# Quantising the ternary layer: two steps of the input rows put on ScalarE, the scaling of the activations on GpSimd, three copies reordered

## What is computed

```python
def _bitlinear(x, w):
    rms = jax.lax.rsqrt(jnp.maximum(jnp.mean(w * w), EPS))
    w_quant = jnp.clip(jnp.round(w * rms), -1.0, 1.0) / rms
    scale = 127.0 / jnp.maximum(jnp.max(jnp.abs(x), axis=-1, keepdims=True), EPS)
    x_quant = jnp.clip(jnp.round(x * scale), -128.0, 127.0) / scale
    return jnp.einsum('bsd,fd->bsf', x_quant, w_quant)
x = x + _bitlinear(gelu(_bitlinear(_layernorm(x), w1)), w2)     # w1: 1024 x 256, w2: 256 x 1024
```

## Time and profile before

| what | value |
|---|---|
| median of 3 runs | 1510.41 us |
| the profiled execution's own time | 1510.13 us |
| its span in the profile | 1508.3 us |
| mean granted TensorE clock, share of full speed | 0.992 |
| span in which the changed lines run | about 1112 to 1160 us |

### The profile page before, as it was taken

The page is one execution under the profiler, slowest core; times in us unless marked ns, Lnnn a source line. Parts: engine busy times, 40 slices in busy tenths (PEclk is TensorE's granted clock), DMA queues, the critical chain, the costliest instruction groups (busy, mean ns, idle before and its releaser), DMA issues. The chain is left out here.

```text
span 1508.3 us, 22223 instructions
## 1 busy us (share of the span) xinstructions
PE 1430.7 (95%) x6910; PEld 1028.8 (68%) x6910; DVE 891.3 (59%) x1934; ACT 768.1 (51%) x2122; POOL 528.0 (35%) x519
## 2 busy tenths in 40 slices
PE   3999998999989999999999999999997999999998
PEld 1678777788875556557878888876764666665656
DVE  7898988898975342323454545354677555553322
ACT  4888888899973211110234444444457555554210
POOL 2667577877762000000434242422110333331000
PEclk9999999999999999999999999999999999999999
DMA  5211000200005511112100000000232000011120
GB/s 202 73 51 60 8 5 2 96 2 1 2 1 220 217 51 51 54 49 91 67 1 1 1 1 1 15 15 1 107 143 102 1 1 1 1 30 42 46 68 18
DMA packets 21303, 71.65 MB, mean 48 GB/s; under 512 B 3858, under 2 KB 6290, under 8 KB 18244
## 3 DMA queue, kind: packets, MB, share of 16 engines
q1 hardware_dynamic: 12980, 57.37, 10.2%
q10 hardware_dynamic: 8208, 12.87, 2.7%
HBM read 69.01 MB, written 1.22 MB: 47 GB/s over the span
## 5 line engine op out<-in xcount | busy, mean ns | idle before, releaser
L1189 ACT ACTIVATE l0f_silu<-bank 128x512 f32<-128x512 f32 x48 | 28.5, 597 | 199.8 <-PE bank L1113 189.7
L827 POOL TENSOR_TENSOR l0a_stepped<-l0a_y,l0a_m 128x512 f32<-128x512 bf16 x64 | 73.9, 1154 | 91.5 <-DVE l0a_m L575 90.4
L1292 DVE TENSOR_TENSOR l0f_product<-l0f_silu,bank 128x512 f32<-128x512 f32 x48 | 32.9, 688 | 123.4 <-ACT l0f_silu L1189 123.3
L855 POOL TENSOR_TENSOR l0a_head_rstd<-l0a_head_var,all_minus_half 128x4 f32<-128x4 f32 x96 | 99.7, 1043 | 7.6 <-DVE l0a_head_var L597 7.6
L767 ACT ACTIVATE l0a_work<-bank,l0a_neg_max 128x128 f32<-128x128 f32 x256 | 90.2, 370 | 1.0 <-DVE l0a_neg_max L610 0.9
L1125 PEld LDWEIGHTS bank<-all_weights_a,l0f_hidden 128*128 128x128 f32 x384 | 72.9, 190 | 25.2 <-issue 17.0
L1721 DVE TENSOR_TENSOR all_weights_a<-bank,all_cols 128x512 f32<-128x512 f32 x64 | 43.9, 690 | 77.9 <-PE bank L1556 45.9
L427 PEld LDWEIGHTS bank<-l0a_k_t,l0a_q_t 128*128 128x128 f32 x512 | 64.0, 191 | 36.7 <-ACT l0a_q_t L753 31.3
L1125 PE MATMUL bank<-all_weights_a,l0f_hidden 128*128 128x256 f32 x384 | 88.9, 379 | 0.0
L2314 PE MATMUL bank<-l3a_f_xn_t,all_weights_b 128*128 128x512 f32 x192 | 86.2, 593 | 0.0
L800 ACT ACTIVATE l0a_work<-l0a_work,l0a_row_inv 128x128 f32<-128x128 f32 x256 | 82.3, 409 | 6.8 <-DVE l0a_row_inv L614 6.7
(11 more groups left out here) (437 smaller groups left out, 3754.1 us busy)
## 6 DMA issues: line engine op xcount, KB each, us to landing
l0f_spread<-l0f_weights ACTq DMA_DIRECT2D x32, 192.0 KB, 2.7
all_weights_a<-in_l_w_q SPq DMA_DIRECT2D x2, 2048.0 KB, 14.3
l0f_spread<-l0f_weights ACTq DMA_DIRECT2D x32, 128.0 KB, 2.8
all_weights_b<-in_l_e_gate_up SPq DMA_DIRECT2D x1, 3200.0 KB, 10.3
all_weights_b<-in_l_e_gate SPq DMA_DIRECT2D x1, 3072.0 KB, 10.0
all_weights_a<-in_l_e_up SPq DMA_DIRECT2D x4, 768.0 KB, 7.0
all_weights_a<-in_l_e_down SPq DMA_DIRECT2D x1, 3072.0 KB, 15.4
l3a_spread<-l3f_weights SPq DMA_DIRECT2D x10, 256.0 KB, 3.5
```

What stands on the lines that cost most here:

```text
L827: done = g.tensor_tensor(stepped[:, 0:n], value, step, ALU.add)
L855: g.tensor_tensor(head_rstd[:, m % 2, :], head_var[:, m % 2, :], res.minus_half[:, 0:HU], ALU.pow)\
```

## The change

ACT gets two steps of `round_in`, for all four pairs (ACT_PAIRS is TILES // 2, which is PAIRS): `normalise_in` (scale rstd, bias -mean x rstd) and `scale_in`. POOL gets the activations' `scale_act`, and the two small scales, and it makes the bias, for which DVE negates the mean. DVE's `round_in` is cut in two, `step_in` (maxima, step, inverse) and a rest. The turning and copying of pairs 2 and 3 are moved forward on PE and ACT, ahead of copies of values, and a one-element Gelu is run early on ACT so that the table of that function is loaded there.

```diff
 PE
                 if t == 3:
                     project_l3_values(6)
+                    turn_in(2)
                     project_l3_values(7)
-                if t % 2 == 1 and t // 2 + 1 < PAIRS:
-                    turn_in(t // 2 + 1)
+                if t == 4:
+                    turn_in(3)
 ACT
             def gelu(t):
-                act.wait_ge(in_q_ready, t // 2 + 1)
+                act.wait_ge(in_scale_ready, t // 2 + 1)
-            def scale_act(t):
-                act.wait_ge(act_inv_ready, t + 1)
-                act.activation(act_rows[t % 4], act_rows[t % 4], ACT.Identity, bias=magic[:],
-                               scale=act_inv[:, t:t + 1]).then_inc(act_scaled, 1)
+            def normalise_in(p):
+                act.wait_ge(in_rstd_ready, p + 1)
+                for t in (2 * p, 2 * p + 1):
+                    done = act.activation(in_rows[:, t, :], res.x[:, t, :], ACT.Identity, bias=in_offset[:, t:t + 1],
+                                          scale=in_rstd[:, t:t + 1])
+                done.then_inc(in_normed, 1)
+            def scale_in(p):
+                act.wait_ge(in_inv_ready, p + 1)
+                if p >= 1:
+                    act.wait_ge(in_q_ready, p)
+                for t in (2 * p, 2 * p + 1):
+                    done = act.activation(in_round[:, t % 2, :], in_rows[:, t, :], ACT.Identity, bias=magic[:],
+                                          scale=in_inv[:, t:t + 1])
+                done.then_inc(in_rounded, 1)
+            act.activation(spare[:], res.minus_half[:, 0:1], ACT.Gelu)
             norm_mix(0)
...
+            normalise_in(0)
+            scale_in(0)
             keep_l3_values(3)
+            normalise_in(1)
             keep_l3_values(4)
+            scale_in(1)
             keep_in(0)
             gelu(0)
+            normalise_in(2)
             keep_in(1)
             gelu(1)
             keep_l3_values(5)
+            scale_in(2)
             for t in range(TILES + 1):
-                if t < TILES:
-                    scale_act(t)
                 if 2 <= t + 2 < TILES:
                     gelu(t + 2)
                 if t == 0:
+                    normalise_in(3)
+                if t == 1:
+                    keep_in(2)
                     keep_l3_values(6)
                     keep_l3_values(7)
                 if t >= 1:
                     keep_act(t - 1)
-                if t % 2 == 1 and (t + 3) // 2 < PAIRS:
-                    keep_in((t + 3) // 2)
+                if t == 1:
+                    scale_in(3)
+                if t == 2:
+                    keep_in(3)
 DVE
+                if p < ACT_PAIRS:
+                    v.tensor_scalar(in_neg[:, pair], res.moments[:, pair, 0], -1.0, None, ALU.mult)
+            def step_in(p):
+                v.wait_ge(in_normed, p + 1)
+                v.tensor_reduce(in_max[:, pair], in_rows[:, pair, :], X, ALU.max, apply_absolute_value=True)
+                v.drain()
+                v.tensor_scalar(in_step[:, pair], in_max[:, pair], T_EPS, 1.0 / 127.0, ALU.max, ALU.mult)
+                v.drain()
+                v.reciprocal(in_inv[:, pair], in_step[:, pair]).then_inc(in_inv_ready, 1)
+            def round_in(p):
+                v.wait_ge(in_rounded, p + 1)
                 if p >= 2:
                     v.wait_ge(in_turned, p - 1)
                 v.tensor_scalar(in_q[:, p % 2, :, :], in_round[:], ROUND_INT, 127.0, ALU.subtract, ALU.min).then_inc(in_q_ready, 1)
-                v.tensor_scalar(act_scale[:, t:t + 1], act_step[:, t:t + 1], ternary.rms[:, 1:2], None, ALU.mult)
             add_to_x(1)
+            step_in(0)
+            open_gate(3)
             round_in(0)
-            open_gate(3)
+            step_in(1)
             add_to_x(2)
             round_in(1)
             add_to_x(3)
+            step_in(2)
             for t in range(TILES + 3):
                 ...
-                if t % 2 == 0 and t // 2 + 2 < PAIRS:
-                    round_in(t // 2 + 2)
+                if t == 0:
+                    round_in(2)
+                    step_in(3)
+                if t == 1:
+                    round_in(3)
 POOL
+            def scale_act(t):
+                g.wait_ge(act_inv_ready, t + 1)
+                g.tensor_scalar(act_rows[t % 4], act_rows[t % 4], act_inv[:, t:t + 1], ROUND_INT, ALU.mult, ALU.add)\
+                 .then_inc(act_scaled, 1)
+            in_rstd_of(0)
+            in_rstd_of(1)
+            in_scale_of(0)
+            in_rstd_of(2)
+            in_scale_of(1)
+            in_rstd_of(3)
+            in_scale_of(2)
+            for t in range(TILES):
+                scale_act(t)
+                act_scale_of(t)
+                if t == 0:
+                    in_scale_of(3)
+                if t == NEXT_MOMENTS:
+                    g.wait_ge(next_var_ready, 1)
+                    g.tensor_tensor(next_rstd[:], next_var[:], res.minus_half[:, 0:1], ALU.pow).then_inc(next_rstd_ready, 1)
```

More of the change, by code:

```diff
@@ L2725, in layer1_adapters_to_layer2 @@
         in_scale = mem.sb("in_scale", [TILES])
+        in_neg = mem.sb("in_neg", [TILES])
+        in_offset = mem.sb("in_offset", [TILES])
+        spare = mem.sb("spare", [1])
+        ACT_PAIRS = TILES // 2
         in_round = mem.sb("in_round", [2, D])
@@ L2784, in layer1_adapters_to_layer2 @@
         in_q_ready = mem.sem("mid_in_q_ready")
+        in_normed = mem.sem("mid_in_normed")
+        in_inv_ready = mem.sem("mid_in_inv_ready")
+        in_rounded = mem.sem("mid_in_rounded")
+        in_scale_ready = mem.sem("mid_in_scale_ready")
+        act_scale_ready = mem.sem("mid_act_scale_ready")
         in_turned = mem.sem("mid_in_turned")
@@ L3372, in add_to_x @@
                 pair = slice(2 * p, 2 * p + 2)
+                if p < ACT_PAIRS:
+                    v.tensor_scalar(in_neg[:, pair], res.moments[:, pair, 0], -1.0, None, ALU.mult)
                 v.tensor_scalar(in_var[:, pair], res.moments[:, pair, 1], T_EPS, None, ALU.add).then_inc(in_var_ready, 1)
[L3375 to L3379, removed]
+            def step_in(p):
+                pair = slice(2 * p, 2 * p + 2)
+                if p < ACT_PAIRS:
+                    v.wait_ge(in_normed, p + 1)
+                else:
+                    v.wait_ge(in_rstd_ready, p + 1)
+                    row_pair(in_rows, in_rstd, p)
+                    v.drain()
                 v.tensor_reduce(in_max[:, pair], in_rows[:, pair, :], X, ALU.max, apply_absolute_value=True)
@@ L3383, in round_in @@
                 v.drain()
[L3384 to L3389, removed]
+                v.reciprocal(in_inv[:, pair], in_step[:, pair]).then_inc(in_inv_ready, 1)
+            def round_in(p):
+                if p < ACT_PAIRS:
+                    v.wait_ge(in_rounded, p + 1)
+                else:
+                    v.drain()
+                    for t in (2 * p, 2 * p + 1):
+                        v.tensor_scalar(in_round[:, t % 2, :], in_rows[:, t, :], in_inv[:, t:t + 1], ROUND_INT, ALU.mult, ALU.add)
+                    v.drain()
                 if p >= 2:
@@ L3490, in _, with in_rstd_of, in_scale_of, act_scale_of @@
                  .then_inc(rstd_ready, 1)
-            for p in range(PAIRS):
+            def in_rstd_of(p):
                 pair = slice(2 * p, 2 * p + 2)
                 g.wait_ge(in_var_ready, p + 1)
-                g.tensor_tensor(in_rstd[:, pair], in_var[:, pair], res.minus_half[:, pair], ALU.pow).then_inc(in_rstd_ready, 1)
-            g.wait_ge(next_var_ready, 1)
-            g.tensor_tensor(next_rstd[:], next_var[:], res.minus_half[:, 0:1], ALU.pow).then_inc(next_rstd_ready, 1)
+                done = g.tensor_tensor(in_rstd[:, pair], in_var[:, pair], res.minus_half[:, pair], ALU.pow)
+                if p < ACT_PAIRS:
+                    g.drain()
+                    done = g.tensor_tensor(in_offset[:, pair], in_neg[:, pair], in_rstd[:, pair], ALU.mult)
+                done.then_inc(in_rstd_ready, 1)
+            def in_scale_of(p):
+                g.wait_ge(in_inv_ready, p + 1)
+                for t in (2 * p, 2 * p + 1):
+                    done = g.tensor_tensor(in_scale[:, t:t + 1], in_step[:, t:t + 1], ternary.rms[:, 0:1], ALU.mult)
+                done.then_inc(in_scale_ready, 1)
+            def act_scale_of(t):
+                g.wait_ge(act_inv_ready, t + 1)
+                g.tensor_tensor(act_scale[:, t:t + 1], act_step[:, t:t + 1], ternary.rms[:, 1:2], ALU.mult)\
+                 .then_inc(act_scale_ready, 1)
+            def scale_act(t):
+                g.wait_ge(act_inv_ready, t + 1)
+                g.tensor_scalar(act_rows[t % 4], act_rows[t % 4], act_inv[:, t:t + 1], ROUND_INT, ALU.mult, ALU.add)\
[15 more added lines that the diff above has]
+                    g.tensor_tensor(next_rstd[:], next_var[:], res.minus_half[:, 0:1], ALU.pow).then_inc(next_rstd_ready, 1)
 PLACES = {
```

1 line of the change is left out of this document (added).

## The result

Eleven timed executions of the changed kernel have the median 1514.54 us (1511.95 to 1516.78), eleven of the kernel before beside them 1510.44 (1509.95 to 1513.03). The ratio is 1.0022, with a 95% interval of 1.0013 to 1.0031: 3.3 us longer, 2.0 to 4.7 (the two medians are 4.1 apart). The profiled execution of the changed kernel took 1512.61 us with a span of 1510.5; that is 2.5 above the profiled execution of before, and among the shorter of the eleven.

The account below looks back on a forecast made before the run. Three engines were taken as nearly full, DVE the fullest. Waits of 8.4 us less 7.7 of removed work gave +0.7, the clock 0.3: 1510.13 + 1.0 = 1511.1 us, range 1506.5 to 1515.0.

Parts of the forecast that it names:

- What DVE loses: Normalising, rounding and in_scale of four pairs and eight act_scale leave DVE, four negated means come: net 7.7 us less.
- The six waits: DVE waits for ACT at round_in(0), step_in(1), step_in(2), round_in(2), step_in(3) and round_in(3): 8.4 us added.
- The ring: Before round_in(3): ACT's scale_in(3) stands behind keep_act(0), which needs DVE's finish_act(0); DVE waits 3.1 us.
- The sign that was named: DVE idle before L3380 and in_q in all four pairs, 8 to 9 us together, longest at pair 3, released by ACT.
- The clock: PE at its lower clock after longer idling makes narrow(0) late for DVE's first add_narrow: up to 0.75 us, taken as 0.3.
- POOL's scaling: The activations' scaling on POOL takes 1.1 us a tile, fitting within one tile's interval of DVE, 2.6 us.
- the third rival: POOL and DVE shut each other out (mutual exclusion); if POOL starts first, +8 us over eight tiles: 1518, chance 0.11.
- The exclusion: At finish_act(t-1) and POOL's scaling of tile t, both released by one inverse: whichever starts first holds up the other.
- the deciding 0.16 us: DVE starts a chained instruction 0.08 us after the last one's start, POOL 0.24 after it, so finish_act starts first.
- Costed at nothing: Forward moves of turn_in and the copies of pairs 2 and 3, and the early Gelu's table load: 0 us.
- the hidden waits: Rival: DVE's waits for ACT mostly hidden, half of them going: 3.5 us gained, 1506.6; chance 0.15.
- Slow POOL: Rival: POOL's scaling at its upper bound, 2.7 us a tile with the small scale, against DVE's 2.6: 1513.8; chance 0.08.

Follow-up runs that it names:

- ring: Changed kernel with ACT's scale_in(3) moved ahead of keep_in(2), so no longer behind keep_act(0); ratio to the kernel before 0.9996 (0.9987 to 1.0006).
- port_swap: Changed kernel with DVE's add_narrow(t-3) put between the inverse and finish_act(t-1); by the ratio +6.3 us (4.4 to 8.3) against the kernel before.
- moves_only: Kernel before with only the forward moves of turn_in and keep_in for pairs 2 and 3; by the ratio +0.8 us (-0.6 to 2.1).
- after_again: The changed kernel run and profiled once more, no edit; median 1515.34 us, kernel before 1512.81, ratio 1.002.
- order: Changed kernel with ACT's list reordered and two DVE steps one tile later, same instructions; median 1507.01 us, ratio to the kernel before 0.997.
- order_rows: `order` with DVE's normalise_next moved ahead of finish_act(3); by the ratio -4.1 us (-5.7 to -2.6) against the kernel before.
- pool_only: Kernel before with only scale_act and act_scale moved to POOL, inputs on DVE as before; by the ratio +2.1 us (0.8 to 3.3).

## Why the prediction was right, and where not

The forecast was 1511.1 us within 1506.5 to 1515.0, as no more than 0.2% away. The median, 1514.54, is in the range but near its end, and the interval of the ratio, 0.13% to 0.31%, straddles the bound. Step by step:

- *What DVE loses, 7.7 us.* About right: on the page DVE's busy time fell by 6.2, where 7.7 less the 0.8 that L3462 grew by is 6.9. Most of the rest is the 0.55 by which six instructions in front of a wait run out in full.
- *The six waits, 8.4.* Right in place, releaser and rank, and in size: counted start to start, as the forecast did, 0.65, 1.12, 0.64, 1.11, 1.78, 2.82 against 0.7, 1.1, 0.6, 1.2, 1.7, 3.1. They are 8.1 in all, and the 0.3 too much is the ring's: there I took the turn at the lower clock's 0.85, and PE took 0.62. The sign that was named, DVE idle for 8 to 9 us in all four pairs, came out at 7.57 us of idle time, and pairs 0 and 1 wait only once each, as the six terms had it.
- *The ring.* Shown by `ring`: that place in ACT's list alone made the wait.
- *The clock, 0.3.* Wrong in its place. I reasoned from the earlier trace rows that longer idle time brings the fall; at the same place the clock was 1.00, and the fall came later (0.77 from 1142 to 1148). Over the 54 us it is 0.97 where it was 0.94. DVE's first `add_narrow` started 0.74 us behind its `finish_act`, where 0.60 is usual, so the term was worth 0.14 at most.
- *POOL's scaling, 1.1.* 1.12 alone. The rate of the Trainium skill (GPSIMD Engine Reference, section 3.1) had given an estimate of 0.88; the measurement decides. That it is held up behind `finish_act` stood only in the third rival, as 0.6 us; it is 0.4, and on the way to the last tile that costs little.
- *The exclusion.* I asked for its effect at `finish_act` and found the deciding 0.16 us right, as `port_swap` shows. **The step that failed is that I asked it of one instruction only.** L3462 is 0.8 us longer beside POOL, no term of my sum. It was offset by three things: the waits were 0.3 too long, the clock's 0.3 mostly did not come, and the changed kernel lacks the stop of 0.35 that the kernel before has. So the block came out at +1.09 where the forecast had +1.0, partly by luck: the last of the three has nothing to do with the working.
- *Costed at nothing.* The moves cost nothing (`moves_only`). But 0.33 on the way and 0.3 outside were no terms of the sum either: together they are more than half of what the block cost.
- *The rest.* Block, way and outside are 1.7 us, and the profile's 2.5 has 0.55 more from code ahead of the block (0.02 in `after_again`, so not the change's) and 0.2 from the next layers. The ratio says 3.3 or, in the second batch, 3.0. Some 1.2 to 1.4 us lie in no part that the profile ties to the change; they are within what the medians of one kernel differ by from one batch to the next, 1510.4 to 1512.8 for the kernel before.

Of the rivals, the hidden waits did not happen as the kernel stands, but `order` shows that they can: its condition, slots of ACT where DVE asks, is met by a list written for it, and it gave 1507.0 where that rival had said 1506.6. Slow POOL is out, at 1.12. Mutual exclusion is real, but at the price of 0.8 and not of 8; with one instruction the other way round it held up four `finish_act` for 2.6 in all.

## What to carry to other kernels

When work leaves the fullest engine for another, count what the fullest engine will then wait for, in the list order of the helper: here 7.7 us of work became 8.1 us of waits, and with the same split of the work the order of the lists, the helper's above all, decided whether it paid. Look first for rings, in which a helper's instruction stands behind one that needs what the waiting engine did last. And where GpSimd gets large SBUF work beside VectorE, list every VectorE instruction of the kind that stood still beside GpSimd's memset in the earlier trace rows, not only the one that starts with it (some will be spared, as `in_q` was), and put such an instruction directly behind what releases GpSimd. Then look whether the engine that uses its result waits for something else as well: in `order_rows` it did, and 0.8 us won on one engine moved nothing.

## What had not been expected of the hardware

- An instruction that is held up by the other engine shows as a longer one, not as idle time: 0.69 becomes 1.42, 0.41 becomes 1.21. The page's waits say nothing of it; only durations by instruction do.
- DVE followed its own inverse after 0.08 to 0.11 us and POOL after 0.24 to 0.27. That margin keeps `finish_act` at 0.69, and in `pool_only` an issue gap of 0.31 us was enough to turn it.
- 28 more POOL instructions added 0.2 us outside of the span, 12 and 16 more nothing; 20 more semaphores added nothing there.
- DVE stood still for 0.42 us in one kernel and for 0.45 at another place in the other, with nothing in the profile that it waited for.
- The granted clock did not follow the length of idle time at one place: 1.91 us of it had 0.50 behind it in the earlier trace rows, 2.14 us had 1.00.
